# Macaron block on one core: clearing moved to SyncE's queue, mask built per tile group, two look-ups moved into the expert turns, ten slabs fetched ahead

## The reference

```python
def _L0_ffn_ref(x, gate_w, gate_b, w1, w2, w3, ws1, ws2, ws3):   # E=64, K=6, CAP=64
    scores = softmax(xf @ gate_w.T)
    _, idx = top_k(scores + gate_b, K)
    weights = take_along_axis(scores, idx, axis=1)
    order = argsort(idx.reshape(-1)); se = flat_e[order]
    pos = arange(T * K) - starts[se]; tok = order // K
    xb = zeros((E, CAP, D)).at[se, pos].set(xf[tok], mode='drop')
    h = silu(einsum('ecd,eid->eci', xb, w1)) * einsum('ecd,eid->eci', xb, w3)
    yb = einsum('eci,edi->ecd', h, w2)
    y = zeros_like(xf).at[tok].add(yb[se, pos] * weights)          # only where pos < CAP
    z = silu(xf @ ws1.T) * (xf @ ws3.T) @ ws2.T
    return y + z

x = x + 0.5 * ffn(layernorm(x))
x = x + linear_attention(layernorm(x), W_qkv, b_qkv, W_out, b_out)   # 16 heads, causal
x = x + 0.5 * ffn(layernorm(x))
```

## Time and profile before

| what | value |
|---|---|
| three timed executions | 594.44, 591.15 and 595.02 us, median 594.44 us |
| the profiled execution | 599.05 us, of which the span shown is 596.8 us |
| DVE busy | 322.3 us (54%) |
| PE busy, by the profile's modelled ends | 365.1 us (61%) |
| POOL busy | 238.0 us (40%) |
| ACT busy | 208.0 us (35%) |
| mean TensorE clock granted | 0.791 of full speed |
| chain that ended last | PE 50%, DVE 23%, issue 9%, DMA 7%, ACT 5%, ACTq 4% |

### The profile page before, as it was taken

One profiled execution on the slowest core, in us unless ns is written; L12 is line 12 of the kernel. 1 busy time (PEld: TensorE's weight loads), 2 busy tenths in 40 slices (PEclk: granted clock), 3 DMA queues, 4 the chain that ended last, 5 costly groups with the idle time before them and its releaser, 6 DMA issues.

```text
span 596.8 us, 14692 instructions
## 1 busy us (share of the span) xinstructions
PE 365.1 (61%) x5808; PEld 271.1 (45%) x5812; DVE 322.3 (54%) x999; ACT 208.0 (35%) x543; POOL 238.0 (40%) x215
## 2 busy tenths in 40 slices
PE   0300763579999900256899999807755599999300
PEld 0300721466657600234688887707523476756300
DVE  6200299343455509915377776466697245454357
ACT  4300761111322300586475767119731012222100
POOL 7000232766788630003222234100507667887600
PEclk9999985557999955567799999855875559999855
DMA  6997930010001049930011112264200010010097
GB/s 202 368 290 249 342 95 4 9 14 7 7 8 9 7 171 405 410 141 1 3 36 35 35 42 47 53 228 142 54 18 13 4 13 7 9 8 6 7 411 288
DMA packets 48585, 62.64 MB, mean 105 GB/s; under 512 B 21572, under 2 KB 36119, under 8 KB 46030
## 3 DMA queue, kind: packets, MB, share of 16 engines
q1 hardware_dynamic: 31715, 43.47, 21.2%
q10 hardware_dynamic: 4547, 17.04, 8.3%
q0 software_dynamic: 12288, 1.70, 2.9%
HBM read 39.53 MB, written 31.46 MB: 119 GB/s over the span
## 4 chain that ended last, share of the span: by engine, by line
PE 50%; DVE 23%; issue 9%; DMA 7%; ACT 5%; ACTq 4%; SPq 1%; POOL 1%; POOLq 0%; DVEq 0%
PE bank L696 7%; PE bank L744 7%; PE upper L830 5%; DVE X L923 4%; PE bank L683 4%; ACTq L286 4%; PE upper L753 4%; PE upper L683 3%; DMA Cb<-planes_d 3%; DVE Eb L1012 3%; ACT A L484 3%; DVE bn L928 2%; DVE Cb L985 2%; PE bank L846 2%; PE bank L815 2%
## 5 line engine op out<-in xcount | busy, mean ns | idle before, releaser
L428 POOL DMA_INDIRECT planes_d<-Bb,put_i x64 | 101.8, 1591 | 41.6 <-issue 20.0
L650 PE MATMUL bank<-ident,A 128*128 128x128 f32 x96 | 23.3, 423 | 120.7 <-ACT A L484 63.4
L442 POOL DMA_INDIRECT A<-rows_d,tok_i x64 | 68.6, 1071 | 51.9 <-DVE put_i L1036 33.0
L456 POOL TENSOR_TENSOR Bb<-Cb,chm 128x576 f32<-128x576 f32 x32 | 36.9, 1184 | 122.8 <-PE upper L875 68.2
L650 PEld LDWEIGHTS bank<-ident,A 128*128 128x128 f32 x96 | 18.9, 227 | 123.7 <-issue 73.3
L409 POOL TENSOR_TENSOR Bb<-Eb,st 128x512 f32<-128x512 f32 x8 | 8.3, 1042 | 106.5 <-DVE st L973 106.5
L1081 DVE TENSOR_SCALAR Bb<-upper,A 64x128 f32<-64x128 f32 x128 | 44.5, 347 | 5.4 <-PE upper L753 4.2
L1069 DVE TENSOR_TENSOR Cb<-Cb,upper 88x512 f32<-88x512 f32 x24 | 16.4, 683 | 43.3 <-ACT Cb L540 35.2
L744 PEld LDWEIGHTS bank<-ring,w1s 128*88 128x88 f32 x256 | 32.2, 183 | 10.1 <-issue 9.8
L753 PE MATMUL upper<-w2s,ring 88*64 88x128 f32 x256 | 30.7, 321 | 9.5 <-issue 7.1
L744 PE MATMUL bank<-ring,w3s 128*88 128x64 f32 x256 | 34.6, 264 | 0.0
(11 more groups left out here) (162 smaller groups left out, 849.8 us busy)
## 6 DMA issues: line engine op xcount, KB each, us to landing
planes_d<-zeros ACTq DMA_DIRECT2D x4, 2048.0 KB, 36.5
planes_d<-zeros SPq DMA_DIRECT2D x4, 2048.0 KB, 21.1
rows_d<-A SPq DMA_DIRECT2D x8, 512.0 KB, 4.1
A<-planes_d SPq DMA_DIRECT2D x4, 1024.0 KB, 5.8
PL<-planes_d SPq DMA_DIRECT2D x4, 1024.0 KB, 9.9
Bb<-planes_d SPq DMA_DIRECT2D x4, 1024.0 KB, 13.6
Cb<-planes_d SPq DMA_DIRECT2D x4, 1024.0 KB, 18.2
w1s<-in_w1T ACTq DMA_DIRECT2D x1, 2816.0 KB
```

The costliest lines, as they stand in the source:

```text
L428: pool.indirect_dma_start(out=planes_d[f], in_=Y[:, s, :], in_offset=None, out_offset=bass.IndirectOffsetOnAxis(ap=put_i[:, s:s + 1], axis=0),
L442: pool.indirect_dma_start(out=GAT[:, t % RING, :], out_offset=None, in_=rows_d, in_offset=bass.IndirectOffsetOnAxis(ap=tok_i[:, t:t + 1], ...
L456: pool.tensor_tensor(out=VX[:, :, :, c, :].rearrange("p q h f -> p (q h) f"), in0=VN.rearrange("p q h f -> p (q h) f"), in1=chm[:, c:c + 1 ...
L650: ins = pe.transpose(bank[g % 2][:, (i % 4) * P:(i % 4 + 1) * P], A[:, i, :], ident[:, :])
```

## The change

In `ffn(0)` the clearing of the planes leaves ACT and becomes SP's work, behind the four score writes. ACT's three weight transfers stay, and no longer wait for the zeros. The mask is computed inside `top`, for one group of eight tiles and all 64 experts at a time, and lies in a free part of Bb. Of the four quarters, the first two are looked up before turn 0 as before; PE's `differences` and `look_up`, ACT's copies and DVE's `table` and `slots` of the other two stand in turns 0 to 3. The first two groups of the shared expert are finished in turns 4 and 5, where they were finished in turns 3 and 5. POOL issues ten gathers before the first add (AHEAD = 10); the ring of buffers still has 15.

```diff
+    AHEAD = 10
-        M = Eb[:, 0:NE * NI // 2].bitcast(BF16).rearrange("p (e i) -> p e i", e=NE)
+        M = Bb[:, NI * NE + 2 * CAP * HE // 2:2 * NI * NE].bitcast(BF16).rearrange("p (e i) -> p e i", e=NE)
@@ shared_part
-            if s in (3, 5):
-                return (s - 3) // 2, 2
+            if s in (4, 5):
+                return s - 4, 2
@@ sync, behind the score writes
+                if f == 0:
+                    sp.wait_ge(zero_set, 1)
+                    clear_planes(sp, 0)
@@ gpsimd
-                    ahead = min(NS, s + RING)
+                    ahead = min(NS, s + AHEAD)
@@ scalar
                 def loads():
-                    act.wait_ge(zero_set, 1)
                     for dst, src in ((w1s, w1T), (w3s, w3T), (w2s, w2T)):
                         act.dma_start(dst[:, :, :], src).then_inc(w_in, 16)
-                    clear_planes(act, 0)
...
+                for h in range(2):
+                    copy_differences(h)
...
+                    if s < 2:
+                        copy_differences(s + 2)
@@ tensor
-                for h in range(NQT):
+                for h in range(2):
                     differences(h)
                     look_up(h)
...
+                    if s == 2:
+                        pe.wait_ge(dr_sb, NQT * (f + 1))
                     if s >= 2:
                         expert_out(s - 2)
+                    if s == 0:
+                        differences(2)
+                        look_up(2)
+                    elif s == 1:
+                        differences(3)
+                    elif s == 2:
+                        look_up(3)
@@ vector, in top(g)
-                    return ins
+                    then(ins)
+                    return dve.tensor_tensor(M[:, :, tiles], RP[:, tiles, 0:NE].rearrange("p i e -> p e i"),
+                                             BI[:, tiles, 0:NE].rearrange("p i e -> p e i"), ALU.not_equal)
-                def mask(h):
-                    ex = slice(HE * h, HE * h + HE)
-                    return dve.tensor_tensor(M[:, ex, :].rearrange("p e i -> p i e"), RP[:, :, ex], BI[:, :, ex], ALU.not_equal)
-                then(mask(0))
                 scan(0)
-                then(mask(1))
+                scan(1)
                 table(0)
-                scan(1)
-                then(mask(2))
                 slots(0)
+                scan(2)
                 table(1)
-                scan(2)
-                then(mask(3))
+                scan(3)
                 slots(1)
                 table(2)
-                scan(3)
-                slots(2)
-                table(3)
-                slots(3)
@@ vector, in the turns
+                    if s == 1:
+                        slots(2)
+                    elif s == 2:
+                        table(3)
+                    elif s == 3:
+                        slots(3)
-                    if s in (2, 4):
+                    if s in (3, 4):
                         for k in range(2):
-                            shared_gate((s - 2) // 2, k)
+                            shared_gate(s - 3, k)
```

More of the change, by code:

```diff
@@ L530, in ffn, with copy_differences @@
                 act.activation(DR[:, :, NI], c32[:, 0:1].broadcast_to([P, NE]), ACT.Copy)
-                for h in range(NQT):
+                def copy_differences(h):
                     act.wait_ge(dr_ps, NQT * f + h + 1)
```

## The result

| | before | after |
|---|---|---|
| median | 594.73 us (4 runs, 591.15 to 596.20) | 557.62 us (4 runs, 556.47 to 559.01) |
| profiled execution, span | 599.05, 596.8 us | 559.01, 557.1 us |
| mean granted clock | 0.791 | 0.778 |

The changed kernel takes 0.9385 of the time, with a 95% interval of 0.9338 to 0.9432. That is 37.1 us faster, inside the range of the prediction and 7.4 us above its number.

A forecast was written before the change was run, and what follows sets the result against it. ACT, held issuing the clearing DMAs, was taken to stall all engines for 40.6 us. Head 40.6, sorting 2 x 1.5 and bodies 2 x 0.3 sum to 44.2 us: 594.44 - 44.2 = 550.2 us, range 540 to 564.

The forecast's parts named there:

- The head: First layer's start: with clearing in SP's queue, PE's second turning of tiles moves from 63.07 to 22.49 us, 40.6 us gained.
- Rows landed: SP's normalised-row writes in the head: weights in at 38 to 40 us, the rows' remaining 1.4 MB until about 48.
- Rival (b): Rows or zeros late in the first layer: first gather 3 us late, zeros up to 9 more; 553 to 562 us, chance 0.14.
- T': Moment the first slots are ready in the changed kernel, forecast at 56.1 us; T is the same moment before, 98.23.
- The zeros: Clearing ahead of POOL's first add: landed about 71 us, may come as late as T' + 26.6 without cost; 0 booked.
- the company of the zeros: First gather landing beside the clearing traffic: 1.2 us added, putting turn 0 at T' + 5.4.
- The mask: New mask per group on DVE: 0.8 us each, bounds 0.69 and 2.37, judged by L1178's strided read.
- The gain in T: DVE's sorting, from the end of the casts to the first slots: 11.7 us becomes 10.2, 1.5 us earlier per layer.
- The bodies: First slots to last add in each layer: slab 5 weighed at T' + 42.1, last add 0.3 us earlier.
- POOL's line: POOL's own work after slab 5's add sets the body's end: last add at T' + 114.9, against T + 115.2.
- rival (c): Gaps in the first turns go: slab 5 weighed some 7 us earlier; 536 us, 543 with a partial effect; chance 0.16.
- The sum: Whole kernel: 40.6 + 2 x 1.5 + 2 x 0.3 = 44.2 us, taken from the median 594.44.

The follow-up runs named there:

- c: The changed kernel with fifteen gathers ahead of the first add instead of ten; 559.18 us, ratio 0.9340 to the kernel before.
- e: The changed kernel with six gathers ahead of the first add instead of ten; 564.35 us, 6.1 us slower than the changed kernel beside it.
- f: The changed kernel with the three weight transfers issued by SP between row and score writes, none on ACT; 564.68 us, 6.4 us slower than the changed kernel beside it.
- j: The changed kernel with w2s in eight transfers and all weight DMAs on SP, ahead of the row writes; 551.50 us, ratio 0.9294 to the kernel before.
- i: The changed kernel with the w2s weight transfer issued as eight transfers of eight experts each; 559.76 us, 2.7 us slower than the changed kernel beside it.
- b: The changed kernel with the clearing back on ACT, so everything but the clearing; 594.28 us, ratio 0.9917 to the kernel before.
- g: The changed kernel with the old masks, each quarter's ahead of its scan; 565.03 us, 6.8 us slower than the changed kernel beside it.
- d: The kernel before with ten gathers ahead instead of fifteen, nothing else; 594.40 us, ratio 0.9917 to the kernel before.
- k: The changed kernel itself, run again for comparison on the chip of i and j; 557.08 us, ratio 0.9373 to the kernel before.
- a: The kernel before with only the first layer's clearing moved to SP, behind the score writes; 560.97 us, ratio 0.9355 to the kernel before.

## Why the prediction was right, and where it was off

**The head: right.** 40.6 us were forecast and 40.8 came, by the mechanism named, and the clearing alone gives the whole result within its interval.

**Rows landed: the step that failed.** "The rows' remaining 1.4 MB [...] until about 48" took the rate of 4.1 us per 0.5 MB from rows that were written alone. The weights, forecast to be in by 38 to 40, still had 22 packets of 32 KB in 48 to 52, and beside w2s the rows landed at 56.3. And I asked only whether POOL's gathers would wait for them. The missing waiter is ACT's L532, through the buffer A. Rival (b) had the late rows, priced as a late gather of 3 us; they came as a T' that is late. The wait can be priced: the first scan started at 50.60 us (404.26 in layer 2), and in layer 2 it is 5.78 us from there to T'; so T' would have been 56.4, and the rows cost 3.6 us. My 56.1 would have been a hit without them. The kernels c and e show the same wait more clearly: their first scans started at 48.38 and 48.40, and T' was still 59.71 and 60.05, so there the rows cost 5.6 and 5.9 us. The kernels f and j, where nobody waits for the rows, have the first scan as early and T' at 54.2; the 2.2 us ahead of the first scan are told of at the end.

**The zeros: size wrong, cost of the late first add right, cost to the gathers missed.** 71 us were forecast, POOL's first add shows 83 to 85. I had said that up to T' + 26.6 they cost nothing: the first add was at T' + 25.5. Three kernels bear that out: with first adds at T' + 24.1, T' + 17.3 and T' + 18.5 (the changed kernel on its second chip, i and j) the last add came at T' + 114.3, 114.7 and 114.8. But I had put 1.2 us into turn 0 for the company of the zeros, and it was about 5: the first gather took 7.2 us to land, and turn 0 came at T' + 8.4 instead of 5.4. In b, whose first body has the same order and no zeros beside it, turn 0 is at T + 3.5, slab 5 is weighed at T + 39.5 instead of T' + 41.2, and the last add is at T + 112.9. So the zeros cost some 2 us there, where I had booked 0.

**The mask: mis-sized.** 0.8 us taken, 1.135 measured, inside the bounds of 0.69 and 2.37. L1178 was the wrong neighbour for the strided read: it reads `upper`, a tensor in PSUM, and the mask reads SBUF. The Trainium skill, "Advanced Engine Details and Errata", section "SBUF Cachelines", says that such an access pays; the trace agrees in the direction (1135 ns against the 685 of L1148, which differs in more than the stride), but as I had applied its rule the mask would have cost at least the 2371 ns of the old one, and it costs half. Four times 0.335 us is 1.3 us per layer. The gain in T can be read in layer 2. From its first MAX8 to T it was 24.22 us (424.23 to 448.45), and now is 22.96 (387.08 to 410.04): 1.3 us less, where 1.5 was forecast. With the mask at 1.135 my sum would have given 0.2, so its other terms were 1.1 us too high. In layer 1 DVE waited for the rows anyway. What g adds is that moving the masks is worth 6.8 us as long as the look-ups are in the turns, because slots(1) comes earlier too. I had counted only T; b and d, which end level, give no sign that masks and look-ups together win anything beyond ten ahead.

**The bodies: POOL's line held, in layer 1 with luck.** T' + 114.9 was forecast and T' + 115.0 came in layer 1, with POOL's steps back to back. But turn 0 was 3.0 us later than forecast and slab 5 still weighed 0.9 us earlier (T' + 41.2 against 42.1), so two errors cancelled. The first add too, held by the zeros until T' + 25.5, gives T' + 114.1 with the 88.6 us of POOL's work behind it. Layer 2 reached T' + 113.2, 1.4 us shorter than before instead of 0.3, since slab 5 was weighed at T' + 39.4 instead of 42.1: rival (c) in part. Its counter-argument, that the gaps are tied to POOL's run of gathers, is what d shows. One count was off by one: with fifteen ahead POOL has 12 gathers behind the add of slab 5, and not 11, so ten ahead adds five there and not six. The sum did not use it.

**The sum.** Head 40.8; lost to the rows and won by the sorting in layer 1, -2.6 together (38.2 for T); body 0.2; sorting 1.3 and body 1.4 in layer 2; and -1.25 between the layers, where from the last add to the first MAX8 it was 210.83 us and is 212.08, with the same instructions. That is 39.8 us, and the spans differ by 39.7, the profiled executions by 40.0. So 4.2 us of the 7.4 are in the sum of 44.2. The other 3.2 come of the base: I took the sum from a median 4.6 us below the profiled execution, and the changed kernel's median is only 1.4 us below its own.

## What to carry to other kernels

A DMA that an engine issues can hold that engine, so long transfers belong in the queue of an engine with nothing to compute, and early in it: with small writes close behind them that others wait for (f) it cost 6.4 us. When small writes share the DMA engines with large loads, count packets and not bytes: beside 32 KB packets the 512-byte rows crawled, and issuing the loads first (j) was worth 5.6 us more. For each late transfer, list every reader and every writer of its buffers, since the one that costs may be an engine that only wants to overwrite the source.

## What the runs showed of the hardware

- **Late completions while POOL issues gathers without a break.** ACT saw a finished product of PE (its end as the profile models it) 6.1 us late beside fifteen gathers and 1.5 us late beside ten, at the same place. The runs tie the delay to the length of the run; what in the chip delays it was not found.
- **w2s moves slowly**, at 107 to 166 GB/s in stretches of 4 us with nothing else large (f), against 387 to 443 for w1s and w3s. It differs in having 88 rows instead of 128 and 32 KB instead of 22 KB each. In rows of 4 KB its queue moved 0.68 to 0.70 MB in 4 us (i), against 0.43 to 0.69 in rows of 32 KB (k), so length is at most a part of it. The 88 rows were not tried apart, and that stays open.
- **PE's matmuls shorten at a moment that I can't place.** The third turning of eight tiles, first in the changed kernel and then in f:

```profile
27.27 1.91 PE L658 MATMUL bank<-ident,A 128*128 128x128 f32 x8
```

```profile
26.49 1.12 PE L656 MATMUL bank<-ident,A 128*128 128x128 f32 x8
```

The granted clock reads 1.00 (the level of 2.4 GHz) in 26 to 28 us in f and in the changed kernel on f's chip alike. In j it is as in f. It does not hang on the weights' coming by SP, for c and e, where ACT issues them as in the changed kernel, have 1.12 and 1.08 us here too, and the clearing alone (a) has 1.04 already for its second turning, at 21.47. So the moment differs between executions, for a reason that stays open. It brings the first MAX8 from 32.5 to 30.2 us (k and j), and is why f and j have T' 2.2 us below 56.4; c and e, which wait for the rows, win nothing by it. So some 2 us of the 6 that f and j gain in T' may be missing in another execution.
- **Issuing blocks at a depth.** ACT issued three weight DMAs in 1.6 us without a stall; with ten, the last held it for 7.42 us, and in the kernel before the fifth, the second clearing, for 20.74.
- **A gather beside the zeros** takes 7.2 us to land, against some 2.3 in the second layer (from 411.02 to turn 0 at 413.36).
